# One register load for four weight offsets, wider late weight loads with at most three in flight, and gathered rows weighed on ScalarE, in a transformer block with 64 routed experts

## The reference, cut to what matters

```python
x = x + _layernorm(_L0_attn_ref(_layernorm(x), ...))
# in _L0_ffn_ref, x as 2048 rows of 128:
rw = _route(x, gate_w, gate_bias)            # (2048, 64), 8 non-zero per row, times 2.5
expert_out = vmap(silu(x @ gw.T) * (x @ uw.T) @ dw.T)   # over 64 experts
routed = einsum('eth,te->th', expert_out, rw)
shared = _mlp(x, Sg, Su, Sd)
x = x + _layernorm((routed + shared))
```

## Time and profile before

| | |
|---|---|
| Median of 3 runs | 691.52 us (691.3 to 692.72) |
| Profiled execution, its own time | 695.79 us |
| Its span | 694.0 us |
| TensorE busy | 541.5 us (78%) |
| VectorE busy | 303.4 us (44%) |
| ScalarE busy | 198.6 us (29%) |
| GpSimd busy | 183.0 us (26%) |
| Mean granted TensorE clock | 0.776 of full |
| Share of the chain that ended last | PE 45%, unknown releasers 17%, VectorE 13%, DMA 9%, issue 9% |

### The profile page before, as it was taken

The page is one execution under the profiler, slowest core; times in us unless marked ns, Lnnn a source line. Parts: engine busy times, 40 slices in busy tenths (PEclk is TensorE's granted clock), DMA queues, the critical chain, the costliest instruction groups (busy, mean ns, idle before and its releaser), DMA issues.

```text
span 694.0 us, 7932 instructions
## 1 busy us (share of the span) xinstructions
PE 541.5 (78%) x2023; PEld 372.1 (54%) x2024; DVE 303.4 (44%) x751; ACT 198.6 (29%) x493; POOL 183.0 (26%) x239
## 2 busy tenths in 40 slices
PE   6999479521578644979899799899998959888886
PEld 5887245310345322646567477577775635555565
DVE  6678634110398212642111111111111439888985
ACT  4798122200122001223222223222222312223223
POOL 6754455777200000000000000000000354656600
PEclk9999558856699977896855955855557889999988
DMA  5470001133266666032222222222221122222211
GB/s 140 186 301 1 4 27 35 53 107 108 66 185 116 62 68 73 23 95 80 69 73 73 69 84 69 69 77 69 69 60 39 49 67 71 73 72 76 77 50 30
DMA packets 71013, 54.07 MB, mean 78 GB/s; under 512 B 6925, under 2 KB 66877, under 8 KB 70973
## 3 DMA queue, kind: packets, MB, share of 16 engines
q1 hardware_dynamic: 66013, 44.85, 25.0%
q0 software_dynamic: 4096, 8.40, 4.0%
q10 hardware_dynamic: 864, 0.33, 0.2%
HBM read 31.53 MB, written 22.02 MB: 77 GB/s over the span
## 4 chain that ended last, share of the span: by engine, by line
PE 45%; another core or an unknown queue 17%; DVE 13%; DMA 9%; issue 9%; SPq 4%; POOL 1%; ACT 1%; POOLq 0%; DVEq 0%; ACTq 0%
PE ps L1889 12%; PE ps L1916 12%; DMA w_raw<-in_w_experts 8%; PE ps L1726 4%; PE ps L1877 3%; PE ps L1901 3%; PE ps L1697 3%; DVE up_w L1266 3%; PE ps L1699 3%; PE ps L1698 3%; SPq L577 3%; DVE total L1371 2%; DVE hid L1276 2%; DVE picked L1369 1%
## 5 line engine op out<-in xcount | busy, mean ns | idle before, releaser
L1697 PE MATMUL ps<-x_hi,w_hi 128*128 128x512 f32 (+1 forms) x184 | 106.1, 577 | 96.4 <-DVE hid L1276 55.1
L728 POOL DMA_INDIRECT picked<-pair_y,slots x64 | 62.4, 976 | 387.1 <-DMA pair_y<-pair_out 368.6
L1697 PEld LDWEIGHTS ps<-x_hi,w_hi 128*128 128x128 f32 x184 | 39.4, 214 | 137.3 <-issue 116.1
L1350 DVE COPY pair_ht<-ps 88x256 f32<-88x256 f32 x64 | 26.9, 421 | 186.2 <-PE ps L1901 186.2
L1889 PE MATMUL ps<-gu_w,pair_xt 128*128 x256 | 94.5, 498 | 7.9 <-issue 7.9
L1726 PE MATMUL ps<-hid,w_raw 128*128 128x512 f32 (+1 forms) x182 | 99.5, 631 | 1.4 <-DVE hid L1276 1.4
L1916 PE MATMUL ps<-down_w,pair_ht 88*128 x256 | 90.1, 453 | 9.9 <-issue 9.0
L978 ACT ACTIVATE ps<-ps 128x512 f32<-128x512 f32 (+1 forms) x92 | 51.3, 562 | 150.6 <-PE ps L1699 108.7
L1266 DVE TENSOR_TENSOR up_w<-ps,route_w 128x512 f32<-128x512 f32 (+1 forms) x92 | 61.1, 664 | 65.7 <-PE ps L1699 29.0
L1916 PEld LDWEIGHTS ps<-down_w,pair_ht 88*128 88x128 f32 x256 | 57.3, 279 | 43.6 <-issue 43.5
L1698 PE MATMUL ps<-x_lo,w_hi 128*128 128x512 f32 (+1 forms) x184 | 77.8, 423 | 0.0
(11 more groups left out here) (215 smaller groups left out, 634.8 us busy)
## 6 DMA issues: line engine op xcount, KB each, us to landing
w_raw<-in_w_experts SPq DMA_DIRECT2D x44, 192.0 KB
pair_x<-zero SPq DMA_DIRECT2D x16, 512.0 KB, 5.4
pair_in<-pair_x SPq DMA_DIRECT2D x32, 256.0 KB, 2.9
pair_y<-pair_out SPq DMA_DIRECT2D x64, 128.0 KB, 1.8
gu_w<-in_w_experts SPq DMA_DIRECT2D x22, 256.0 KB
down_w<-in_w_experts SPq DMA_DIRECT2D x11, 256.0 KB
pair_x<-x_rows,slots POOLq DMA_INDIRECT x64
picked<-pair_y,slots POOLq DMA_INDIRECT x64
```

Of the source, the lines that this page charges most:

```text
L728: g.indirect_dma_start(picked[:, t % 3, k, :], None, pair_y, bass.IndirectOffsetOnAxis(ap=slots[:, t, k:k + 1], axis=0)).then_inc(s_pick[t ...
L1350: v.tensor_copy(pair_ht[:, u % 2, :], ps[0:HID, 5, 0:2 * P]).then_inc(s_pht, 1)
L1697: t_.matmul(out_, hi, mhi, start=start, stop=False)
```

## The change

1. **Offsets.** unit_gu and unit_d become one table, unit_at, with four numbers for each turn of the burst: gate/up offsets of the two tiles of unit i and down offsets of the two tiles of unit i - 2. unit_offsets loads the four into registers with one call at the start of the turn, and the runtime bounds check of each value is left out. The layout of gu_w follows the loads, and factor gets other numbers (three more affine selects), so that an expert's offset counts in the new layout.
2. **Late weights.** A gate/up load takes two sets with gate and up together, runs of 1 KB in place of 512 bytes; a down load takes one of 8 hidden rows for two sets and all rounds, so 11 partitions eight apart in place of 8 neighbouring ones. There are 22 and 16 of them. Each load from the fourth on waits for the third before it (three semaphores).
3. **Orders.** Quad 3's input and logits (E3, F3, Y3, X3) stand earlier in the four orders, ranking stages X1 to X3 and Y0 to Y3 later; on GpSimd the first scatter (I0) follows E3.
4. **Pair weights.** The 24 pieces of pair_weights go from the steps of round 1 into VectorE's part of the burst, one behind every second unit.
5. **Combine.** ScalarE multiplies each gathered row by its weight (weigh_pairs, eight activations a tile), at the same place in the steps as combine; VectorE waits for it and sums by three additions of halves in place of one multiplication and one reduction.

```diff
-        unit_gu = sb("unit_gu", [1, P], I32)
-        unit_d = sb("unit_d", [1, P], I32)
+        unit_at = sb("unit_at", [1, BURST + 2, 2, UNIT_TILES], I32)
...
-        gu_w = sb("gu_w", [P, ROUNDS, 2, E * PACK])
+        gu_w = sb("gu_w", [P, ROUNDS, SETS * 2 * P + P])
...
-            "E1 T34 F1 T35 C31 T36 Z0 T37 C32 C33 Z1 D0 E2 F2 D1 Z2 X0 Z3 X1 D2 X2 D3 X3 E3 F3 "
-            "Z4 Z5 G2 D4 N20 D5 N21 Z6 Z7 D6 Z8 D7 Z9 D8 Z10 D9 Z11 D10 G3 D11 N30 N31 Z12 Z13 "
+            "E1 T34 F1 T35 C31 T36 Z0 T37 C32 C33 Z1 D0 E2 F2 D1 Z2 X0 E3 F3 Z3 D2 X1 Z4 D3 X2 "
+            "Z5 G2 D4 X3 N20 D5 N21 Z6 Z7 D6 Z8 D7 Z9 D8 Z10 D9 Z11 D10 G3 D11 N30 N31 Z12 Z13 "
...
-            "F2 M1 E2 J2 X3 R3 I0 E3 I1 M2 F3 I2 I3 J3 I4 I5 I6 M3 "
+            "X3 F2 M1 E2 J2 R3 E3 I0 I1 M2 F3 I2 I3 J3 I4 I5 I6 M3 "
...
-            "Z0 Z1 R2 Z2 Z3 R3 Z4 Z5 Z6 Z7 O0 Z8 Z9 O1 Z10 Z11 P0 Y1 Y2 "
+            "Z0 Z1 R2 K7 Z2 Z3 R3 Z4 Z5 Z6 Z7 O0 Z8 Z9 O1 Z10 Z11 P0 Y1 Y2 "
...
-                    for half in range(2):
-                        yield (gu_w[:, r, half, :].rearrange("p (c n) -> p c n", c=SETS),
-                               w_experts[r, :, :, P * half:P * half + P].rearrange("c h n -> h c n"))
-                for r in range(ROUNDS):
-                    yield (down_w[PACK * r:PACK * r + PACK].rearrange("k (c j) h -> k c j h", c=SETS),
-                           w_experts[r, :, :, WD:WD + P].rearrange("c (j k) h -> k c j h", k=PACK))
+                    for c in range(0, SETS, 2):
+                        yield (gu_w[:, r, WD * c:WD * c + 2 * WD].rearrange("p (c n) -> p c n", c=2),
+                               w_experts[r, c:c + 2, :, 0:WD].rearrange("c h n -> h c n"))
+                for k in range(PACK):
+                    for c in range(0, SETS, 2):
+                        e = PER_CHUNK * c
+                        rows = w_experts[:, c:c + 2, :, WD:WD + P].rearrange(
+                            "r c (j k) h -> r k (c j) h", k=PACK)
+                        yield (down_w[k:HID:PACK, e:e + 2 * PER_CHUNK, :], rows[:, k])
...
                 for _ in range(min(n, len(late))):
+                    done = LATE - len(late)
+                    if done >= 3:
+                        sp.wait_ge(s_late[done % 3], 16 * (done // 3))
                     to, src = late.pop(0)
-                    sp.dma_start(to, src).then_inc(s_late, 16)
+                    sp.dma_start(to, src).then_inc(s_late[done % 3], 16)
...
+                for c in range(1, SETS):
+                    link(g.affine_select(out=factor[:, 0:1], in_=factor[:, 0:1],
+                                         compare_op=ALU.not_equal, fill=float(PACK + P),
+                                         base=1 - PER_CHUNK * c, pattern=[[0, 1]],
+                                         channel_multiplier=1))
...
+            def weigh_pairs(t):
+
+                b = t % 3
+                if t == 0:
+                    act.wait_ge(s_pw, 1)
+                act.wait_ge(s_pick[b], 16 * CHOSEN * (t // 3 + 1))
+                for k in range(CHOSEN):
+                    ins = a.activation(picked[:, b, k, :], picked[:, b, k, :], ACT.Copy,
+                                       scale=pair_w[:, t, k:k + 1])
+                ins.then_inc(s_wgt, 1)
...
+                at = r * PER_ROUND + k
+                if at in COMBINE_AT:
+                    weigh_pairs(COMBINE_AT[at])
...
-                v.tensor_copy(unit_gu[:], ps[0:1, 6, P:2 * P]).then_inc(s_tab, 1)
-                v.tensor_copy(unit_d[:], ps[0:1, 6, 2 * P:3 * P]).then_inc(s_tab, 1)
+                gate, down = [ps[0:1, 6, P * i:P * i + PAIR_TILES].rearrange("p (u t) -> p u t", t=UNIT_TILES)
+                              for i in (1, 2)]
+                v.tensor_copy(unit_at[:, 0:BURST, 0, :], gate)
+                v.tensor_copy(unit_at[:, BURST:, 0, :], gate[:, 0:2, :])
+                v.tensor_copy(unit_at[:, 0:2, 1, :], down[:, 0:2, :])
+                v.tensor_copy(unit_at[:, 2:, 1, :], down).then_inc(s_tab, 1)
...
+                    if i % 2 == 1 and 3 <= i < 3 + 6 * ST:
+                        pair_weights(i // 2 - 1)
...
-                dve.wait_ge(s_pick[b], 16 * CHOSEN * (t // 3 + 1))
+                dve.wait_ge(s_wgt, t + 1)
...
-                link(tt(picked[:, b], picked[:, b],
-                        pair_w[:, t, :].unsqueeze(2).to_broadcast([P, CHOSEN, C]), ALU.mult))
-                ins = v.tensor_reduce(total[:, own, :], picked[:, b].rearrange("p k c -> p c k"),
-                                      AX.X, ALU.add)
-                ins.then_inc(s_red, 1)
+                link(tt(picked[:, b, 0:4], picked[:, b, 0:4], picked[:, b, 4:8], ALU.add))
+                link(tt(picked[:, b, 0:2], picked[:, b, 0:2], picked[:, b, 2:4], ALU.add))
+                tt(total[:, own, :], picked[:, b, 0], picked[:, b, 1], ALU.add).then_inc(s_red, 1)
...
-                if r == 1:
-                    pair_weights(k)
...
+            def unit_offsets(i):
+
+                _, at = nc.values_load_multi_w_load_instructions(
+                    unit_at[0:1, i].rearrange("p a t -> p (a t)"), engines=[mybir.EngineType.PE],
+                    min_val=0, max_val=C * (E - 1),
+                    skip_runtime_bounds_check_because="63 rows of 0 or 1, times 8, 128 or 136")
+                return at[0:UNIT_TILES], at[UNIT_TILES:]
...
-                pe.wait_ge(s_late, 16 * 3 * ROUNDS)
-                pe.wait_ge(s_tab, 2)
-                pair_gate_up(0)
+                for b in range(3):
+                    pe.wait_ge(s_late[b], 16 * len(range(b, 2 * ROUNDS + 2 * PACK, 3)))
+                pe.wait_ge(s_tab, 1)
+                pair_gate_up(0, unit_offsets(0)[0])
                 for i in range(BURST + 1):
+                    gate_at, down_at = unit_offsets(i + 1)
                     if i + 2 < BURST:
                         turn_pairs(i + 2)
                     if i + 1 < BURST:
-                        pair_gate_up(i + 1)
+                        pair_gate_up(i + 1, gate_at)
                     if i < BURST:
                         turn_pair_hidden(i)
                     if i >= 1:
-                        pair_down(i - 1)
+                        pair_down(i - 1, down_at)
```

More of the change, by code:

```diff
@@ L321, in build @@
         s_scat = [sem(f"pairs_scattered{t}") for t in range(ST)]
-        s_late = sem("late_weights_loaded")
+        s_late = [sem(f"late_weights_loaded{b}") for b in range(3)]
         s_pin = [sem(f"pair_tiles_loaded{b}") for b in range(4)]
@@ L335, in build @@
         s_red = sem("pairs_summed")
+        s_wgt = sem("pairs_weighed")
+        s_pw = sem("pair_weights_ready")
         s_fvar = sem("sparse_variance_ready")
@@ L625, in _ @@
                         sp.wait_ge(s_rw, SETS * len(DENSE))
-                        sp.wait_ge(s_tab, 2)
+                        sp.wait_ge(s_tab, 1)
                         sp.wait_ge(s_ysh, 2)
@@ L1092, in _ @@
                     split_hi((ROUNDS - 1) * SETS + k)
+                elif what == "K":
+                    weigh_pairs(k)
                 elif what == "P":
@@ L1312, in keep_units, with pair_weights @@
                 dve.wait_ge(s_unit, 1)
-                v.tensor_copy(unit_gu[:], ps[0:1, 6, P:2 * P]).then_inc(s_tab, 1)
-                v.tensor_copy(unit_d[:], ps[0:1, 6, 2 * P:3 * P]).then_inc(s_tab, 1)
-            def pair_weights(t):
-                if t == 0:
-                    dve.wait_ge(s_route, len(SPARSE))
-                link(tt(found[:], place[:, t, :].unsqueeze(1).to_broadcast([P, CHOSEN, E]),
-                        chosen[:, t, :].unsqueeze(2).to_broadcast([P, CHOSEN, E]), ALU.is_equal))
-                link(tt(found[:], found[:],
-                        weights[:, t, :].unsqueeze(1).to_broadcast([P, CHOSEN, E]), ALU.mult))
-                link(v.tensor_reduce(pair_w[:, t, :], found[:], AX.X, ALU.add))
-                if t + 1 == ST:
-                    link(v.tensor_scalar(pair_w[:], pair_w[:], ROUTED_SCALE, None, ALU.mult))
+                gate, down = [ps[0:1, 6, P * i:P * i + PAIR_TILES].rearrange("p (u t) -> p u t", t=UNIT_TILES)
[4 more added lines that the diff above has]
+                v.tensor_copy(unit_at[:, 2:, 1, :], down).then_inc(s_tab, 1)
+            def pair_weights(i):
+                t = i // 3
+                if i == 0:
+                    dve.wait_ge(s_route, len(SPARSE))
+                if i % 3 == 0:
+                    link(tt(found[:], place[:, t, :].unsqueeze(1).to_broadcast([P, CHOSEN, E]),
+                            chosen[:, t, :].unsqueeze(2).to_broadcast([P, CHOSEN, E]), ALU.is_equal))
+                elif i % 3 == 1:
+                    link(tt(found[:], found[:],
+                            weights[:, t, :].unsqueeze(1).to_broadcast([P, CHOSEN, E]), ALU.mult))
+                else:
+                    link(v.tensor_reduce(pair_w[:, t, :], found[:], AX.X, ALU.add))
+                if i + 1 == 3 * ST:
```

(16 more changed lines are left out.)

5 lines of the change are left out of this document (3 added, 2 removed), and 4 rows, old and new, of tables (ACT_ORDER, DVE_ORDER).

## The result

The changed kernel takes **497.62 us** (median of 4 runs, 497.04 to 498.41) beside 691.41 for the kernel before (four runs): a ratio of 0.7201, 95% interval [0.7178, 0.7223]. I had forecast 541 and a range of 503 to 608, so the direction was right and the size was not: 43 us more went than I said. The profiled execution has a span of 495.3 us, 198.7 less than the 694.0 of before, where I had 151.

The account below looks back on a forecast made before the run. TensorE's sequencer was taken to set the burst, VectorE and slow down loads the dense rounds. Terms -106 - 42 - 3 = -151 on the profiled 695.8 gave 544.8, 541 us as median; range 503 to 608.

Parts of the forecast that it names:

- The burst: Burst of 64 two-tile units: fewer offset loads and no checks cut 233 us to 127, -106; bounds -137 and -41.
- handovers between engines: Burst units: cost a floor leaves out, so 1.8 us a unit at full clock was taken, above the 1.46 floor.
- rival B: Burst: the load of four costs four reads, only checks vanish, 179 us for the burst, 593 us total; chance 0.1.
- rival A: Burst stays at 1.2 GHz: 64 units of 3.0 us, 192 us, 606 us total; chance 0.2.
- Late and pair weights: Dense rounds 1 to 4: faster late loads and pair weights moved under the burst, -42 us; bounds -10 and -50.
- rival C: Late loads do not do what they should, leaving 33 us of stall: 566 us, up to 573; chance 0.1.
- Rival D: Slower than before: SP waits so long for down loads, about 11 us each, that the burst starts late; chance 0.02.
- Orders: First stages: reordering removes at most one wait of some us on GpSimd, -3 us; bounds +10 and -20.
- Weighing on ScalarE: Late-round combines: VectorE saves 1.8 us a tile but waits 2.1 to 2.5 more for ScalarE, 0 us; bounds -12, +8.
- An unchanged 13 us per tile: Combines in the late rounds: sign of being right, VectorE idling 2 us before its sums, tile time staying 13 us.
- The stage before 186 us: Stretch from 134 to 186 us: the 52 us hole ends with the scatters, whatever comes before; SP's releaser unnamed.

Follow-up runs that it names:

- e1: Kernel before with only the offsets change (one load of four, no bounds check): 510.73 us beside 648.5 for the kernel before, ratio 0.7905.
- e4: Changed kernel with one load of four offsets kept and the bounds checks added back: 519.75 us beside 648.5 for the kernel before, ratio 0.8057.
- e6: Changed kernel with the old late weight loads (gate/up and down) and no limit of three: 536.35 us beside 693.0 for the kernel before, ratio 0.7775.
- e7: Changed kernel with the 24 pieces of pair weights back in round 1: 509.86 us beside 693.0 for the kernel before, ratio 0.7371.
- e16: Changed kernel with only the eleven old down loads back, new gate/up packets and limit kept: 486.59 us beside 645.0 for the kernel before, ratio 0.7528.
- e11: Changed kernel with the four old stage orders: 502.48 us beside 691.05 for the kernel before, ratio 0.7256.
- e8: Changed kernel with weighing and reducing back on VectorE, no ScalarE activations: 510.43 us beside 693.0 for the kernel before, ratio 0.7355.
- e9: Changed kernel with GpSimd waiting for landing after every four scatters from the 15th on: 464.44 us beside 691.05 for the kernel before, ratio 0.6702.
- e3: Changed kernel with each offset loaded singly, without bounds checks: 515.0 us beside 648.5 for the kernel before, ratio 0.7978.
- e2: Changed kernel with each offset loaded singly and bounds-checked: 594.83 us beside 648.5 for the kernel before, ratio 0.9221.

## Why the prediction was wrong, point by point

**The burst, -106 said, -135 measured (-138 in e1).** This is the step that failed, and in it the size alone: the mechanism (loads and checks in TensorE's sequencer) is shown by e1 to e4. The term was 54 units at 1.8 us and 10 at 3.0, 127 us, where the stage took 98. I had a floor of 1.46 us a unit and added 0.34 for "handovers between engines", then ten units at half clock. The unit is 1.48 us and the clock was 1.00 in the whole stage. 54 units x 0.3 and 10 x 1.5 make 31 us, which is the miss of 29 to within 2. Handovers cost next to nothing. The other stages missed by 10 and 11.7 us the same way and by 3 the other: 47.7 in the profiled executions. In the medians it is 43, since the profiled execution of before lay 4.3 us above its median and that of the changed kernel 0.6 below. In the code each of the four pieces of a turn belongs to a different tile pair, so the other engines have a turn for their answer; ScalarE with 60.9 and VectorE with 57.4 of the 98 us left room. With a floor of 1.46 and two engines at 60%, the floor was the better guess. The load of four was 0.33 us, nearer to one load (0.30) than my 0.4, and rival B is dead. So is rival A: the clock was 1.00.

The page "DMA: Bandwidth & Descriptors" of the Trainium skill (Latency and other measured facts) gives a floor of about 600 ns for a tensor load. The rows show 0.30 us for one number and 0.33 for four; the measurement decides. The 13 us more that I had estimated from the Trainium skill's figure are not there.

**Late and pair weights, -42 said, -52 measured.** Undone one at a time they are worth 34 (e6) and 8 (e7), so both sizes were right and rival C is dead. I had left 8 us of the stage for low clock and stalls; the stage has neither (clock 0.98, TensorE busy throughout). The 10 us between the sum of the two and the stage were not taken apart further. The reason given, eight neighbouring partitions, fits e16, which does not separate it from the size and the order of a load. By the page "SBUF — State Buffer" of the Trainium skill (Door 1: The DMA port swizzle) such a load reaches two ports, an estimate of 54 GB/s, and eleven partitions eight apart reach seven. The traces agree: e16 has the stall back with the old down loads alone, and the changed kernel has none. Rival D, SP held for 11 us by each load, fell far off: it is 2.5 to 2.9 us for three.

**Orders, -3 said, 0 to within some 5 us measured** (e11): within the bounds of +10 and -20.

**Weighing on ScalarE, 0 said, -8.4 measured** (e8), within my bound of -12 but not where I put it. Here a wait was put too long, and with it nothing seemed to be gained. The sum of VectorE's work was right (1.41 us: 0.69, 0.43 and 0.29). The wait was not: I had 2.1 to 2.5 us and the row shows 0.86. ScalarE needs 2.44 us for the eight, not 3.1: each lasts 0.39 us and not the 0.50 of the earlier trace rows, and from start to start it is 0.30. And VectorE ends its own product 2.1 us after the silu began (395.10 to 397.21), not 1.5. In this tile no cast stands in front; in the tile at 408.14 one does, and the wait is 0.83 all the same. Six of the eight tiles have a wait of this size. "An unchanged 13 us per tile" is 12.4. The last 3 us of the stage's 11.7 were not taken apart.

**The stage before 186 us** I read rightly as unchanged, but I left its cause open ("a releaser that the profile does not name") and took it for a matter of the scatters' end. I also read the earlier trace rows wrongly: 125.9 us cannot lie in a stretch of 52. One wait of 102.2 us ends at 146.7 us and had begun at 44.4; of the three, only its last 13 us and one of 14.7 us that ends at 187.2 belong to the stretch. Closing the stretch is worth 38 us in this same kernel (e9).

## What to carry to other kernels

Work out the floor of the bound engine for a pipelined inner loop. In this one the other engines filled about 60% of it and the floor was the forecast to make. Registers that steer tiles should be loaded many at once and without a run-time check where the values are sure: in this burst, doing one of the two alone left 0.9 us a unit, and both together took 2.1. When the profile shows an engine that waits for a releaser it does not name, compare the end of the work it needs with its start; a gap of 10 us in a stretch of unbroken indirect DMAs on GpSimd went away with a break after every four or eight, and the breaks cost nothing measurable where the gap was absent.

## What the runs showed that I had not expected

- On some chips, engines that wait for TensorE go on up to 14 us late while GpSimd issues a long unbroken run of indirect DMAs (some 50 at 1.27 us); on another (e3) the same copy goes on after 0.04 us beside the same run. It goes with the difference between 691 and 645 to 648 us for the kernel before, and of the 47 us between 502 and 455 for the changed one the breaks take 38 away; the other 9 stand, by the traces, at the first 24 gathers, which are unbroken, too. Breaks of 1.9 us after four, or a wait after eight, remove it. How the two are joined in the hardware no run here shows.
- TensorE held 2.4 GHz through 159 us in which it was shown busy 70% (e4). In e2, shown busy 73% while at full clock, it was granted a mean of 0.56 over the 233 us of the burst.
- A register load of four numbers takes 0.33 us, of one 0.30.
- The changed kernel with pauses takes 464 us where it took 502, and 455 on the other kind of chip. It is the fastest of the kernels run, 0.67 of before on the one kind and 0.71 on the other.
